# GATv2 attention on one core: the path over edges in steps of one row of 128 edges in place of two

## What is computed

```python
x_l = (x @ W_l).reshape(n, H, C)
x_r = (x @ W_r).reshape(n, H, C)
e = (ea @ W_e).reshape(-1, H, C)
m = leaky_relu(x_l[src] + x_r[dst] + e, 0.2)
alpha = einsum('ehc,hc->eh', m, att)
amax = segment_max(alpha, dst, num_segments=n)
expa = exp(alpha - amax[dst])
denom = segment_sum(expa, dst, num_segments=n)
a = expa / (denom[dst] + 1e-16)
out = segment_sum(x_l[src] * a[:, :, None], dst, num_segments=n)
```

## Time and profile before

| | |
|---|---|
| median of three runs | 2233.2 us (2232.06 to 2237.89) |
| the profiled execution | 2248.54 us, span 2246.7 us |
| PE busy | 1820.9 us (81%) |
| DVE busy | 1327.8 us (59%) |
| ACT busy | 1066.6 us (47%) |
| GpSimd busy | 847.4 us (38%) |
| attention, first to last slope | 854.7 to 2150.1 us, 214 groups |

### The profile page before, as it was taken

The page is one execution under the profiler, slowest core; times in us unless marked ns, Lnnn a source line. Parts: engine busy times, 40 slices in busy tenths (PEclk is TensorE's granted clock), DMA queues, the critical chain, the costliest instruction groups (busy, mean ns, idle before and its releaser), DMA issues. The chain is left out here.

```text
span 2246.7 us, 35285 instructions
## 1 busy us (share of the span) xinstructions
PE 1820.9 (81%) x10692; PEld 1277.1 (57%) x10692; DVE 1327.8 (59%) x3113; ACT 1066.6 (47%) x2345; POOL 847.4 (38%) x891
## 2 busy tenths in 40 slices
PE   6777799979999973677878878878888778888776
PEld 2667665567888741345545555545555545555564
DVE  6999777664333363755555555555555555555585
ACT  1889867545423450234434444434444444444465
POOL 2000000010000016766666666666666666666500
PEclk9555599989999996799898998888989998999887
DMA  3000000005300012323233223323233233323311
GB/s 104 24 2 1 8 2 1 5 25 151 91 1 6 1 44 69 90 77 82 77 80 83 78 80 82 82 76 84 77 81 81 77 81 82 83 76 82 79 35 29
DMA packets 132195, 133.01 MB, mean 59 GB/s; under 512 B 28888, under 2 KB 102063, under 8 KB 132015
## 3 DMA queue, kind: packets, MB, share of 16 engines
q1 hardware_dynamic: 104238, 73.55, 11.4%
q0 software_dynamic: 27776, 57.20, 10.3%
HBM read 125.84 MB, written 4.82 MB: 58 GB/s over the span
## 5 line engine op out<-in xcount | busy, mean ns | idle before, releaser
L2275 POOL DMA_INDIRECT rows<-x_l,src x856 | 821.3, 959 | 477.1 <-issue 224.3
L2400 ACT ACTIVATE bent<-psum 128x512 f32<-128x512 f32 x214 | 127.4, 596 | 606.6 <-DMA near<-e_ends 340.6
L2361 PE MATMUL psum<-both,node_hot 128*128 128x144 f32 x1712 | 308.6, 323 | 66.3 <-issue 56.0
L2361 PEld LDWEIGHTS psum<-both,node_hot 128*128 128x128 f32 x1712 | 265.9, 213 | 143.0 <-issue 127.2
L2548 DVE TENSOR_TENSOR acc<-acc,psum 128x144 f32 x428 | 127.0, 297 | 278.4 <-remote 198.3
L2293 PEld LDWEIGHTS psum<-hot,x_r_parts 128*128 x1284 | 133.5, 104 | 249.0 <-issue 228.6
L2293 PE MATMUL psum<-hot,x_r_parts 128*128 128x256 bf16 x1284 | 201.2, 296 | 90.3 <-DVE hot L2454 31.1
L2415 ACT ACTIVATE apart<-iota,rel 128x128 bf16<-128x128 f32 x856 | 270.6, 388 | 1.4 <-PE psum L2361 1.4
L2313 PE MATMUL psum<-bent,att_heads 128*128 128x512 f32 x428 | 244.7, 661 | 9.0 <-DVE bent L2458 6.1
L2296 PE MATMUL psum<-edges,w_e 128*128 128x512 f32 x428 | 239.5, 642 | 0.7 <-issue 0.7
L2458 DVE TENSOR_TENSOR bent<-psum,bent 128x512 f32<-128x512 f32 x214 | 146.9, 686 | 127.9 <-issue 117.8
(11 more groups left out here) (347 smaller groups left out, 2400.3 us busy)
## 6 DMA issues: line engine op xcount, KB each, us to landing
rel_row<-e_rel_rows SPq DMA_DIRECT2D x107, 256.0 KB
edges<-edge_t SPq DMA_DIRECT2D x428, 32.0 KB
rows<-x_l,src POOLq DMA_INDIRECT x856
edge_part<-edge_t SPq DMA_DIRECT2D x40, 320.0 KB, 3.1
new<-e_new_before SPq DMA_DIRECT2D x26, 64.0 KB
new<-e_new_behind SPq DMA_DIRECT2D x26, 64.0 KB
ht<-x SPq DMA_DIRECT2D x6, 256.0 KB, 2.8
x_l<-rows SPq DMA_DIRECT2D x4, 320.0 KB
```

The lines of the kernel that those rows point to most:

```text
L2275: e.indirect_dma_start(rows[:, g % ring, j * ROW:(j + 1) * ROW], None, k.xl, bass.IndirectOffsetOnAxis(ap=src[:, at:at + 1], axis=0)).then ...
L2361: final = e.matmul(to, near_hot[:, at, j, :], both[:, at, j, :], start=j % 2 == 0, stop=j % 2 == 1)
```

## The change

A step becomes one row of 128 edges. 806 rows and 24 changes of block make 830 steps; a group is four steps that may lie in four blocks, so there are 208 groups (832 gathers for 856), padded to 208. The tables have seven chunks of 128 steps instead of four, with gathers and rows half as wide, and DVE's search is done in two parts. In the attention stage `begin` has twelve matmuls of 128 columns in place of six of 256; SP loads the edge features in four transfers per group in place of two; registers are loaded every two groups in place of every four. The sums of a row are no longer added to those of its pair in PSUM: each row's sum stands by itself, three rows to a bank, and DVE adds them to `acc` one by one, by trios of rows. A batch's factor is 8 wide instead of 136 and is spread by DVE, in two multiplications.

```diff
         assert self.csteps <= 2048
         self.strides = -(-self.csteps // STRIDE)
-        self.groups = -(-(self.pairs + self.nb - 1) // 2)
+        self.groups = -(-(self.tiles + self.nb - 1) // 4)
         self.padded = -(-self.groups // 16) * 16
 
     def rows(self, b):
...
     k.ident = k.sb(k.ctx, "ident", [P, P])
     k.eps = k.sb(k.ctx, "eps", [P, 1])
     k.edge_sum = k.sb(k.ctx, "edge_sum", [P, 1])
     with ExitStack() as scope:
         def sb(name, shape, dt=F32):
             return k.sb(scope, name, shape, dt)
-        src_pairs, dst_pairs = (io[x].rearrange("(g k) e -> g (k e)", k=2) for x in ("src_rows", "dst_rows"))
-        groups = Path(k, scope, "e", io["dst_last"], 2, src_pairs, dst_pairs, 7, s.nb, 2 * s.padded)
+        groups = Path(k, scope, "e", io["dst_last"], 1, io["src_rows"], io["dst_rows"], 7, s.nb, 4 * s.padded)
         en = groups.nch
         steps = en * P
...
@@ -568,8 +579,10 @@
                 e.memset(k.eps[:, :], EPS).then_inc(*v.up())
                 c.vector_numbers(e)
                 ended = groups.ends_of_tiles(e, v, c)
+                groups.find(e, v, c, ended, range(3))
                 c.vector_dst(e)
-                groups.vector(e, v, c, ended)
+                groups.find(e, v, c, ended, range(3, en))
+                groups.vector(e, v, c)
                 c.vector_src(e)
                 c.empty(e, 0)
                 e.memset(guard[:, :], -5.0).then_inc(*ends_ready.up())
...
@@ -679,8 +693,8 @@
                 e.dma_start(near[:, 0, :], ends_flat[1, 0:P, :]).then_inc(*near_here.up(16))
                 e.dma_start(near[:, 1, :], ends_flat[0, 2:P + 2, :]).then_inc(*near_here.up(16))
                 e.wait_ge(moved.sem, moved.at(4))
-                e.dma_start(k.e_src, srct[:, 0:2 * s.padded, :].rearrange("p g k -> p (g k)")).then_inc(*stored.up(16))
-                e.dma_start(k.e_rel, relt[:, 0:2 * s.padded, :].rearrange("p g k -> p (g k)")).then_inc(*stored.up(16))
+                e.dma_start(k.e_src, srct[:, 0:4 * s.padded]).then_inc(*stored.up(16))
+                e.dma_start(k.e_rel, relt[:, 0:4 * s.padded]).then_inc(*stored.up(16))
                 for q, r in chunks:
                     e.dma_start(rel_rows[q * P:q * P + r, :], rel16[0:r, q, :]).then_inc(*stored.up(16))
                 for j in range(2):
...
         return next(b for b in plan if b.first <= g < b.over)
 
-    def adds(u):
-
-        return 2 * (u + 1) + sum(b.first <= u for b in plan)
+    def adds(row):
+
+        return row + 1 + 2 * sum(4 * b.first <= row for b in plan)
+
+    def trios(u):
+
+        return [m for m in range(-(-4 * groups // 3)) if min(3 * m + 2, 4 * groups - 1) // 4 == u]
...
@@ -2222,20 +2241,17 @@
             @block.sync
             def _(e):
                 e.wait_ge(loaded.sem, loaded.at(here))
-                pair = Registers(k, ENGINE.SP, regs[0:1, 0, :], 2 * groups, s.pairs)
-                pairs_t = io["edge_t"].rearrange("q (v r) e -> (q v) r e", v=2)
-
-                def rows_of_pair(at):
-                    return pairs_t[bass.ds(at, 1), :, :].rearrange("o (t d) e -> d (o t) e", t=2)
+                tile = Registers(k, ENGINE.SP, regs[0:1, 0, :], 4 * groups, s.tiles)
+                rows_t = io["edge_t"].rearrange("q (v r) e -> (q v) r e", v=4)
 
                 def fetch(g):
                     r, r2, old = g % slots, g % slots // 2, g - slots
-                    two = pair.at(2 * g), pair.at(2 * g + 1)
+                    four = [tile.at(4 * g + j) for j in range(4)]
                     if g >= edge_slots:
                         e.wait_ge(products.sem, products.at(g - edge_slots + 1))
-                    for j, at in enumerate(two):
-                        e.dma_start(edges[0:DE, g % edge_slots, j * 2 * P:(j + 1) * 2 * P].rearrange("d (t e) -> d t e", t=2),
-                                    rows_of_pair(at)).then_inc(*edge_here[g % edge_slots].up(16))
+                    for j, at in enumerate(four):
+                        e.dma_start(edges[0:DE, g % edge_slots, j * P:(j + 1) * P],
+                                    rows_t[bass.ds(at, 1), :, :].rearrange("o d e -> d (o e)")).then_inc(*edge_here[g % edge_slots].up(16))
                     if g % 2 == 0:
                         if old >= 0:
                             e.wait_ge(hots.sem, hots.at(old + 2))
...
@@ -2280,18 +2296,18 @@
             def _(e):
                 def begin(g):
                     two, z = g % 2, z_banks[g % 2]
-                    blocks = [block_of.at(2 * g + j) for j in range(2)]
-                    due_parts = min(2 * g + 1, s.nb - 1) // 5
-                    if due_parts > min(max(2 * g - 1, 0), s.nb - 1) // 5:
+                    blocks = [block_of.at(4 * g + j) for j in range(4)]
+                    due_parts = min(4 * g + 3, s.nb - 1) // 5
+                    if due_parts > min(max(4 * g - 1, 0), s.nb - 1) // 5:
                         e.wait_ge(split.sem, split.at(4 * due_parts))
                     e.wait_ge(hots.sem, hots.at(g + 1))
                     if g >= 2:
                         e.wait_ge(leaky.sem, leaky.at(g - 1))
-                    for j in range(2):
-                        half = slice(j * 2 * P, (j + 1) * 2 * P)
+                    for j in range(4):
+                        quarter = slice(j * P, (j + 1) * P)
                         for q in range(3):
-                            e.matmul(z[:, half], row_parts.parts[:, bass.ds(blocks[j], 1), q, :].rearrange("p o f -> p (o f)"),
-                                     hot[:, two, half], start=j + q == 0, stop=False)
+                            e.matmul(z[:, quarter], row_parts.parts[:, bass.ds(blocks[j], 1), q, :].rearrange("p o f -> p (o f)"),
+                                     hot[:, two, quarter], start=j + q == 0, stop=False)
                     e.wait_ge(edge_here[g % edge_slots].sem, edge_here[g % edge_slots].at(edge_lap(g)))
                     e.matmul(z, w_e[:, :], edges[:, g % edge_slots, :], start=False, stop=False).then_inc(*products.up())
 
...
@@ -2344,25 +2360,27 @@
                                     k.ident[0:b.lines, 0:b.lines]).then_inc(*back.up())
 
                 def sum_rows(u):
-                    at, bank = u % deep, sum_banks[u % 2]
-                    if u >= 2:
-                        e.wait_ge(added.sem, added.at(adds(u - 2)))
-                    if u in begun:
-                        i = begun[u].i
-                        e.wait_ge(spread.sem, spread.at(3 * i + 3))
-                        e.matmul(bank[:, 2 * wide:2 * wide + scaled], is_first[:, :], factor[:, :], start=True, stop=False)
-                        e.matmul(bank[:, 2 * wide:2 * wide + scaled], others[:, :], ones[:, :],
-                                            start=False, stop=True).then_inc(*factors.up())
+                    at = u % deep
                     e.wait_ge(hot_scalar.sem, hot_scalar.at(u + 1))
                     e.wait_ge(filled.sem, filled.at(u + 1))
                     e.wait_ge(weighted.sem, weighted.at(u + 1))
                     for j in range(4):
-                        to = bank[:, j // 2 * wide:(j // 2 + 1) * wide]
-                        final = e.matmul(to, near_hot[:, at, j, :], both[:, at, j, :], start=j % 2 == 0, stop=j % 2 == 1)
+                        row = 4 * u + j
+                        m, third = divmod(row, 3)
+                        bank = sum_banks[m % 2]
+                        if m >= 2 and third == 0:
+                            e.wait_ge(added.sem, added.at(adds(3 * m - 4)))
+                        if j == 0 and u in begun:
+                            i = begun[u].i
+                            e.wait_ge(spread.sem, spread.at(3 * i + 3))
+                            e.matmul(factors_in(bank), is_first[:, :], factor[:, :], start=True, stop=False)
+                            e.matmul(factors_in(bank), others[:, :], ones[:, :], start=False, stop=True).then_inc(*factors.up())
+                        final = e.matmul(bank[:, third * wide:(third + 1) * wide], near_hot[:, at, j, :], both[:, at, j, :],
+                                         start=True, stop=True)
                     final.then_inc(*totals.up())
 
                 e.wait_ge(loaded.sem, loaded.at(here))
-                block_of = Registers(k, ENGINE.PE, regs[0:1, 1, :], 2 * groups, s.nb - 1)
+                block_of = Registers(k, ENGINE.PE, regs[0:1, 1, :], 4 * groups, s.nb - 1)
                 begin(0)
                 for t in range(len(due)):
                     if t < groups:
@@ -2441,11 +2459,8 @@
                 e.wait_ge(loaded.sem, loaded.at(here))
                 e.tensor_reduce(begins[:, :, :], by_pair[:, :, :, :], AX.X, ALU.min).then_inc(*ready.up())
                 heads = k.ident[0:HEADS, 0:HEADS]
-                e.tensor_copy(mask[:, 0:D].rearrange("p (h c) -> p h c", c=CH),
-                                   heads.rearrange("p (h o) -> p h o", o=1).to_broadcast([HEADS, HEADS, CH])).then_inc(*v.up())
```

(31 more changed lines are left out.)

89 lines of the change are left out of this document (49 added, 40 removed).

## The result

The changed kernel takes 2259.7 us (median of four, 2255.9 to 2262.0), the one before 2234.8 beside it: ratio 1.011, interval 1.009 to 1.012. It is slower by 25 us, where +44 and 2277 were forecast, and it lies inside the forecast's own range. The direction was right; but two terms of the working were far off in opposite directions, so that the sum came out near is in good part luck. On another chip the same kernel does not lose at all (e9).

What follows compares the result with a forecast made beforehand. No engine was full; the loop through PE, late with its instructions, was taken to bound attention. Terms -36 + 3 + 71 + 6 = +44 took 2233.2 to 2277 us; whole range 2195 to 2385, the forecast's own 2240 to 2330.

Steps and rivals of the forecast that it cites:

- the forecast's own range: Whole kernel: moderately slower, 2240 to 2330 us, given a chance of 0.42.
- the twelve matmuls: PE's first matmuls of an attention group: +0.42 us, 81% of it on the path, +71 us over 208 groups.
- the end: After the last slope PE waits for DVE's adds: 0.88 us more per group, +12 us at most, +6 taken.
- Its own signs: Attention's middle: slopes 6.3 to 6.4 us apart, PE busy 0.85 or more, PE's `acc` waits near 4 us per 1000.
- a sign of a wrong forecast: Attention stage: PE's stalls put down to issue falling instead of growing would show the forecast wrong.
- Fewer groups: Attention loop: 214 groups become 208, each of the six worth 6.0 us, -36 us.
- Tables: Table stage: fourteen one-row gathers for eight of two, 21 stores for 12; bounds 0 and +8, value +3 us.
- my lower bound: PE's twelve matmuls at 0.055 us apart, from rows of 125 columns, take 0.93 us: +0.11 us per group.
- The wait in the middle: PE's sums needing the adds of group u - 1: bounds 0 and +2.3 us per group, 0 taken.
- The faster one: Attention loop keeps 6.0 us per group, extra PE and DVE work falls in idle time: -33, 2200 us; chance 0.28.
- The beginning late: First groups need parts of x_r sooner: +10 to +20 us upon any other, alone 2215 us; chance 0.04 alone.
- The stalls of PE: Attention's middle: PE's sequencer late with instructions, perhaps at 256-instruction block crossings; no term, only in the upper bound.

Runs made afterwards that it cites:

- e9: The changed kernel again, no edit, on a quick chip: 2036.4 us against 2039.2 for the kernel before, ratio 0.9985.
- e1: The kernel before, again with no edit, for a second profile: 2232.3 us.
- e11: The kernel before with eight slots for gathered rows in place of six, on a quick chip: 2037.7 us, ratio 1.000.
- e2: The kernel before with a group's first six matmuls cut into twelve of 128 columns, nothing else: 2246.0 us, ratio 1.006.
- e3: The kernel before with PE's sums of a group waiting for the adds of group u - 1 instead of u - 2: 2260.8 us, ratio 1.012.
- e7: The kernel before with each add of 144 columns cut into two of 72, four per group, on a quick chip: 2042.0 us, ratio 1.002.
- e4: The changed kernel with each add behind the last slope following the next group's weighing in DVE's queue: 2254.3 us, ratio 1.010.
- e12: The changed kernel with PE's signal to DVE at each trio of rows, DVE's order unaltered, on a quick chip: 2028.6 us, ratio 0.9946.
- e5: The changed kernel with PE's signal at each trio and adds earlier in DVE's order at the end, on a quick chip: 2023.9 us, ratio 0.992.
- e6: The changed kernel with the second and third part of x_r split before the first group, on a quick chip: 2033.4 us, ratio 0.997.
- e10: The changed kernel with DVE's order at the end, the signal at each trio and the early x_r split together, quick chip: 2023.5 us, ratio 0.9925.

## Why the prediction was right, and where it was not

The total was right because one term that was far too large (the twelve matmuls, +71) stood beside one that was far too small (the end, +6), and a middle that lost more than the matmuls explain. Its direction holds for chip A only. Its own signs spoke against it: the groups are 6.04 us apart and not 6.3 to 6.4, PE's busy share of the middle is 0.82 and not 0.85 or more, and PE's idle time put down to issue fell from 98.1 us (e1) to 33.4 in 1000 (part of it now stands at the wait for adds), which I had named as a sign of a wrong forecast.

*Fewer groups, -36.* Right by the pace: 6 x 6.01 on chip A, and 6 x 5.08 = -30 on the others (1081.9 / 213 in e11). No run changes the number of groups alone.

*Tables, +3.* PE's first counting matmul starts at 60.4 us for 55.6 in e1, +4.8. Over all profiles it starts at 55.6 to 58.9 us with the old tables and at 57.9 to 60.4 with the new, on average 2.3 us later. So the size was right.

*Twelve matmuls, +71.* This is the step that failed most. Alone they cost 14 us (e2), 12.6 of them between first and last slope. The price was wrong first: I had taken 0.10 to 0.12 us from one matmul to the next, whatever its columns, so +0.72 us for six more, and took the middle between that and my lower bound. Queued, the twelve stand 0.056 us apart and take as long as the six (e2). That is the pace of my lowest price, from the matmuls of 125 columns in the earlier trace rows. It is under the Trainium skill's 81 ns, which the prediction cites; here the measurement decides. I had discounted those rows because no register instruction stands between them; it makes no difference that shows. The share was wrong too: I counted 81% as on the path because PE is busy 81% of the time, and a busy share is no share of the path. Of the middle's +25 us the matmuls make 12 and the later wait about 4 (0.02 us per group over the whole stretch, e3); the adds are hidden on chip B (e7). The other 8 or so no run takes apart, and they are less than two profiles of one kernel differ by there.

*The end, +6, at most +12.* Measured +26.6. I priced the number of adds alone, which e7 puts at 8 us. The lost slack, which I had looked for in the middle, is worth 20.8 us there (e3). The two make 28.4 by single runs, where the changed kernel shows 26.6 on chip A and 24.3 on the others. Here the groups come two to a turn, so that in e3 the adds of u - 1 belong to the same turn as the sums of u and are only issued in the next one. In the changed kernel, though, issuing the adds earlier brings only 2 us (e4). 8 us are that DVE may not begin a bank's adds before PE has done the whole group, while PE waits for these adds to go on (e12). With both edits the end is still 52.4 us for 39.7 (e5, e11); what makes that rest stays open. I had read the row that shows PE waiting for adds just there and did not ask what one group less of slack would do to it.

One rival was not run: 208 groups are 26 full batches, while 214 leave a last batch of six. So eight groups in place of six are due behind the last batch's pieces, with one more turn in which no group is summed. From their first weighing to the end of the sums the last six take 11.6 us in e1, 1.9 each, and the last eight 29.0 us after, 3.6 each:

```profile
2156.56 0.67 DVE L2528 TENSOR_TENSOR both<-rows,psum 128x512 f32<-128x512 f32 x1
```

```profile
2166.09 0.69 DVE L2543 TENSOR_TENSOR both<-rows,psum 128x512 f32<-128x512 f32 x1 [0.84 <-PE psum L2359]
```

So most of it is a slower exchange and not two more groups; and e3, with 214 groups, has its 20.8 us without the full batch.

*The wait in the middle, 0.* Right by size: the wait appears (116 us of PE, in 82 waits, after) and is nearly absorbed: 0.02 us per group in e3.

*The rivals.* The faster one had the mechanism of the middle: the loop nearly keeps its pace. It missed the end. "The beginning late" was forecast as +10 to +20 on top of another, and the first slope is 11.1 us later, 4.8 of it from the tables. But it scatters: 864.6 and 859.4 us with the changed beginning on chip A, where the old one has 853.5 to 857.8, and 853.6 to 857.8 on chips B, where the old one has 851.9 and 855.5. What is left of it beside the tables is not settled. e6 and e10 speak against the splitting as the cause.

*The stalls of PE*. I took them for late code. On chips B the same instructions go without such stalls: there PE's sums of a group read x8 in 1.14 or 1.25 us with a slope every 5 us, and "issue" before their weight loads is never over 0.2 us in the middle of e7, before those of the first matmuls never over 0.7, where e1 has up to 1.8 and 3.4. So the amount of code does not make the stalls by itself, and the Trainium skill ("Runtime: NRT & Kernel Launch", instruction fetch mechanics), that the crossing of a block is mostly hidden, agrees with these rows of chips B. Whether code comes later on chip A no run tells. What does make PE stall on chip A, with the granted clock at 0.90 where the others have 0.99 to 1.00, stays open. Whether the lower clock is the cause or the companion of the stalls, these runs do not tell.

## What to carry to other kernels

Price a change that shortens the slack between two engines where they run closest, that is in the stretch in which a loop is drained, and not only in the even middle: 14 groups at the end lost 26 us here, and 208 in the middle lost 25. Price a matmul from rows of the nearest number of columns: twelve of 128 took as long as six of 256 here. A busy share says nothing of what added work costs; a run with that work alone does. Where a buffer is refilled by parts, signal by the same parts: one signal per bank in place of one per group was worth 8 us at the end on chips B.

## What the runs showed of the hardware that I had not expected

The same kernel takes 2232 us on one chip and 2039 on two others, nearly all by the attention stage (its groups take 5.95 and 5.03 us in e1 and e11), with the granted clock at 0.90 and 1.00 there. The stages before it are alike: the first slope is at 853.5 and 851.9 us. So a change that trades gathers for PE's and DVE's work was worth +1.1% on chip A and -0.15% on one of the others. And where PE waits often, its rows get longer too: in e3's end the granted clock is 0.58, and PE is busy 37.4 us for about the records that took 24.6 in e1:

```profile
2142.00:2198.00 56.00, 37.37 (x150) 30.69 (x148) 29.05 (x82) 24.21 (x68) 0.00 (x0) 0.58 0.09 25
```

But the clock alone does not make the end long. Here are the ends of the first profile of before and of e11:

```profile
2150.00:2185.00 35.00, 27.10 (x149) 23.59 (x148) 28.52 (x81) 23.89 (x68) 0.00 (x0) 0.80 0.14 39
```

```profile
1933.80:1973.50 39.70, 32.35 (x159) 26.83 (x157) 29.10 (x81) 24.00 (x67) 0.00 (x0) 0.70 0.09 25
```

At 0.90 (e1) and at 0.80 the end takes 35.1 and 35.4 us, and at 0.70 it takes 39.7 in e11, where the changed kernel takes 61.7 at 0.69.
